# Dense steps up to sixty slots ahead of their target, in place of sixteen, in a hand-planned FFN-attention-FFN kernel

## What is computed

```python
x = x + 0.5 * ffn(layernorm(x))      # r * (relu(k)^2 W_v), r = sigmoid(xr W_r), k = xk W_k
x = x + attention(layernorm(x))      # 16 heads of 16, rotary q and k, causal softmax
x = x + 0.5 * ffn(layernorm(x))
```

## Time and profile before

| | us |
|---|---|
| median of 3 runs | 3071.79 (3069.86 to 3072.07) |
| the profiled execution | 3073.15 |
| its span, first to last instruction | 3071.4 |
| TensorE products busy in it | 2945.7 |
| VectorE busy | 2531.8 |
| ScalarE busy | 2216.2 |
| POOL busy | 1573.0 |
| mean granted TensorE clock | 0.989 of full |

### The profile page before, as it was taken

One profiled execution on the slowest core, in us unless ns is written; L12 is line 12 of the kernel. 1 busy time (PEld: TensorE's weight loads), 2 busy tenths in 40 slices (PEclk: granted clock), 3 DMA queues, 4 the chain that ended last, 5 costly groups with the idle time before them and its releaser, 6 DMA issues.

```text
span 3071.4 us, 56193 instructions
## 1 busy us (share of the span) xinstructions
PE 2945.7 (96%) x18245; PEld 1670.0 (54%) x18245; DVE 2531.8 (82%) x7302; ACT 2216.2 (72%) x4802; POOL 1573.0 (51%) x2190
## 2 busy tenths in 40 slices
PE   6899999999999999999999999999999999999997
PEld 4454555555555555555555555555555555555444
DVE  3788887888888888888888888888888898888872
ACT  4477776777777777777777777777777777777764
POOL 5455454555555554465555555455454554555323
PEclk9899999999999999999999999999999999999998
DMA  3433443443444343453443443434453543443421
GB/s 100 81 67 73 76 101 64 88 83 76 91 72 91 76 85 74 80 99 65 88 79 71 102 77 81 84 73 85 78 98 61 101 81 66 96 76 76 84 58 39
DMA packets 202584, 245.48 MB, mean 80 GB/s; under 512 B 68405, under 2 KB 104245, under 8 KB 202293
## 3 DMA queue, kind: packets, MB, share of 16 engines
q1 hardware_dynamic: 202293, 241.90, 40.3%
HBM read 53.48 MB, written 51.38 MB: 34 GB/s over the span
## 4 chain that ended last, share of the span: by engine, by line
PE 70%; DVE 21%; issue 3%; ACT 3%; POOL 1%; SPq 1%; DMA 1%; POOLq 0%; DVEq 0%; ACTq 0%
PE ps_y L954 14%; PE ps_s L923 13%; PE ps_m L933 12%; PE ps_d L1010 6%; PE ps_d L1013 6%; PE ps_d L1007 6%; DVE ps_m L1162 5%; PE ps_d L1019 4%; PE ps_d L1000 3%; DVE mx_sb L1165 3%; PE ps_d L1023 2%; PE ps_d L961 2%; DVE ka_sb L1187 2%; DVE qb_sb L1220 2%; ACT pt_sb L1049 1%
## 5 line engine op out<-in xcount | busy, mean ns | idle before, releaser
L1049 ACT ACTIVATE pt_sb<-ps_s 128x512 f32<-128x512 f32 (+1 forms) x3039 | 1460.3, 491 | 676.1 <-PE ps_s L923 645.7
L1162 DVE CUSTOM_DVE_ANT_0 ps_m<-ps_m,mask_sb 128x128 f32<-128x128 f32 (+3 forms) x2048 | 995.5, 497 | 275.7 <-PE ps_m L933 252.9
L933 PE MATMUL ps_m<-kr_sb,qr_sb 96*128 96x512 bf16 (+3 forms) x3072 | 1003.4, 330 | 55.5 <-DVE mx_sb L1162 44.8
L923 PE MATMUL ps_s<-qr_sb,kr_sb 99*128 99x512 bf16 (+1 forms) x3039 | 994.5, 330 | 23.1 <-ACT pt_sb L1049 14.3
L1165 DVE TENSOR_REDUCE mx_sb<-ps_m 128x1 f32<-128x512 f32 x1024 | 700.9, 684 | 130.6 <-PE ps_m L933 124.7
L1294 POOL TENSOR_SCALAR_AFFINE_SELECT pt_sb<-pt_sb 128x512 f32<-128x512 f32 x512 | 339.8, 664 | 820.3 <-ACT pt_sb L1049 819.6
L954 PE MATMUL ps_y<-pt_sb,v_sb 128*32 128x512 f32 (+3 forms) x6144 | 591.5, 495 | 4.5 <-POOL pt_sb L1294 3.3
L923 PEld LDWEIGHTS ps_s<-qr_sb,kr_sb 99*128 99x128 bf16 x3039 | 292.6, 96 | 440.9 <-issue 238.0
L933 PEld LDWEIGHTS ps_m<-kr_sb,qr_sb 96*128 96x128 bf16 x3072 | 302.2, 98 | 381.4 <-DVE mx_sb L1162 114.5
L1007 PE MATMUL ps_d<-ka_sb,wk_sb 128*128 128x256 f32 x1024 | 314.5, 394 | 2.4 <-DVE dif_sb L1199 2.0
L1019 PE MATMUL ps_d<-axn_sb,wqk_sb 128*128 128x256 f32 x1024 | 310.5, 389 | 3.8 <-ACT axn_sb L1091 3.8
(11 more groups left out here) (96 smaller groups left out, 3537.2 us busy)
## 6 DMA issues: line engine op xcount, KB each, us to landing
kr_sb<-part_sb SPq DMA_DIRECT2D x378, 128.0 KB, 4.5
qr_sb<-part_sb SPq DMA_DIRECT2D x378, 128.0 KB, 5.0
y_way<-yt_sb SPq DMA_DIRECT2D x128, 256.0 KB, 2.7
sw_sb<-qb_sb SPq DMA_DIRECT2D x496, 64.0 KB, 2.0
x_sb<-x SPq DMA_DIRECT2D x64, 256.0 KB, 4.1
yn_sb<-y_way SPq DMA_DIRECT2D x64, 256.0 KB
den_sb<-r_way SPq DMA_DIRECT2D x64, 256.0 KB
out<-x_sb SPq DMA_DIRECT2D x64, 256.0 KB, 2.2
```

The costliest lines, as they stand in the source:

```text
L923: eng.matmul(score_bank(slot)[:, 0:width], kr_sb[0:KR + NP, n % RS, j, kb * P:(kb + 1) * P], qr_sb[0:KR + NP, n % RS, j, q0:q0 + width], s ...
L933: eng.matmul(ps_m[:, u % NM, 0:width], qr_sb[0:KR, n % RS, j, i * P:(i + 1) * P], kr_sb[0:KR, n % RS, j, piece * QC:piece * QC + width], s ...
L1049: eng.activation(pt_sb[:, buffer, j, column:column + width], score_bank(slot)[:, 0:width], ACT.Exp, scale=SCALE).then_inc(exped, 1)
L1162: eng.tensor_tensor_reduce(ps_m[:, u % NM, 0:width], ps_m[:, u % NM, 0:width], mask_sb[:, m0:m0 + width], 1.0, -3e38, ALU.add, ALU.max, be ...
```

## The change

`EARLY`, the number of slots by which a dense step of rank group 2 may stand ahead of its target, goes from 16 to 60. It is used in one place, `step()`, and holds for both planners. Nothing else is changed.

```diff
     UNIT = 4 * CH / GHZ
     TICK = 900
-    EARLY = 16
+    EARLY = 60
```

## The result

| | before | after |
|---|---|---|
| median, same chip, 4 runs each, us | 3071.93 (3069.86 to 3074.42) | 3130.95 (3129.51 to 3132.89) |
| span of the profiled execution | 3071.4 | 3131.2 |
| mean granted TensorE clock | 0.989 | 0.983 |

The change makes the kernel slower by 59.0 us: ratio 1.0195, interval [1.0182, 1.0207].

A forecast was written before the change was run, and what follows sets the result against it. The prediction took the slot-by-slot interlock of TensorE's and VectorE's lists as the bound. Its terms, 0 - 10.8 + 3.8 - 4.2 + 2.9 = -8.3 us, gave a forecast of 3064 us, range 3036 to 3096.

The forecast's parts named there:

- Step 1: Steady batches: holes filled before the second FFN reopen later at about the same unit price; change 0.
- Rival A: Dense steps: POOL and VectorE collide more, +22 us, 3087 us; L1187 mean over 0.70 us for, under 0.68 against; chance 0.24.
- Step 2: Dense work moves up to 44 slots ahead, 36 units from the last batches into the start, 0.30 us each: -10.8 us.
- Steps 3 and 4: Start: moved FFN units partly uncovered on VectorE, +3.8 us; second pair's rope steps, -4.2 and +2.9 us.
- Step 4 (b): Start: second pair's rope swap, cosine, sine and addition may delay VectorE's first maximum: 0 to +5.8, taken as +2.9 us.
- 4 (a): Start: earlier rope product 4 lets the L862 DMAs releasing the first score begin sooner, before 82 us: -4.2 us.
- Rival B: Whole kernel: dependences hold steps in place, or costs in the start eat the shift; +2.1 us, 3074 us; chance 0.22.
- Rival C: Steady batches: runs of slots without a unit come apart, letting VectorE catch up; 33 us faster, 3032 us; chance 0.12.

The follow-up runs named there:

- the two holds: POOL's dense steps wait, from one slot before VectorE's five short maxima steps, until these end: before 3043.97 us; sixty from slot 48 only 3044.34 us.
- at 32: Bound of 32 from slot 48 on, sixteen in the start, with POOL's wait one slot before the five maxima steps: 3056.05 us against 3069.86 before.
- the bound by clocks: Kernel before with sixty slots only in the planner by clocks (slot 48 on), sixteen kept in the start: 3121.93 us against 3071.23.
- the hold in after: Changed kernel with POOL's dense steps waiting, from one slot before the five short maxima steps, until these end: 3059.23 us against 3069.76 before.
- the hold and sixteen in the start: Sixty from slot 48 on only, with POOL's wait one slot before the five maxima steps: 3044.34 us against 3069.76 before.
- the rope steps alone: Kernel before with sixty slots in the start for the rope steps only, sixteen for everything else: 3088.25 us against 3069.86.
- the FFN steps alone: Kernel before with sixty slots in the start for FFN and attention norm steps only: 3078.18 us against 3069.86.
- the fills: Kernel before with twelve write-only POOL fills of a spare tile per head group, beside the five maxima steps: 3137.44 us against 3069.86.
- the reading steps: Kernel before with six short POOL products per head group that read SBUF, beside the five maxima steps: 3173.46 us against 3069.76.

## Why the prediction was wrong

**Step 1 ("steady batches: 0") is the step that failed.** It argued by units: as many holes open as are filled, at one price. That part held between sixteen and sixty, as the two holds show (365.5 against 365.8 us for two batches), though not at 32, 12 us worse. What it left out is that the list also fixes what POOL does while VectorE runs its rows of short steps. The ten batches 4 to 13, which it put at 0, grew by 42.7 us; the bound by clocks cost 50.7 us in all, and with the hold in both kernels 0.4 us of it is left.

**Rival A had the mechanism and the sign, and the wrong place.** It priced collisions where they were easy to see, in L1187 and L1193, and set the mean of L1187 as its sign. That mean is 0.648 us, under the 0.68 that spoke against A, while A was happening in five lines that it left out, as small steps of 128x32 or less. What the change does to such a step reaches TensorE: VectorE's next maximum stands behind the last of the five in its queue, and TensorE's next product waits for it. (That a dense mix has slack in front of its user was not measured.) At +45 us of VectorE the price was also twice the +22 given. The Trainium skill's page "SBUF — State Buffer", section "SBUF: two separate sides", says that the shared port goes to whoever starts first, for its whole instruction, where VectorE's has two SBUF inputs and POOL's reads SBUF. By that rule a step of 0.18 us costs as much as the POOL step ahead of it; the traces agree, with 1.25 us beside a POOL step of 1.28.

**Step 2 (shift, -10.8)** had the count and about the right size per unit. The lists have 35 more units ahead of slot 0, and 28 fewer in batch 14, at 0.30 us each with the hold in after (0.35 with the hold and sixteen in the start). There -8.5 us would have come, but only -2.0 showed in after, which the hold turned into -8.5. The end of the kernel gained almost nothing more (-1.0 us).

**Steps 3 and 4 (+3.8, -4.2, +2.9: +2.5 in all)** were mis-sized. Step 4 (b) looked at one chain, POOL's cosine for rope product 4, and put the worst at 5.8 us for the first maximum. It came 19.4 us later, as rope steps 4 and 5 and a whole FFN chunk got ahead of it. The gain of 4 (a) did not come: the L862 DMAs began at 104.17 us, not before 82, since the maxima that they need were late. Slot 0 came 26.3 us later. With sixty in the start alone the units already done returned 16.3 us of it in batch 0, which step 2 counted only at the end, and the net was +10.4 us. No run parts steps 3 and 4 cleanly: the rope steps alone cost 18.4 us, the FFN steps alone 8.3.

Rival B (no change) fell with the 59 us, though its thought that the start eats the shift was near. Rival C's holes came apart only in part (by the lists a steady batch has 8 slots in runs of five or more, where before had 25 in two batches), and its 33 us are not there even with the blocking gone: the bound alone is worth 0.4 us then.

## What to carry to other kernels

A reordering is also a change of what runs side by side. Before you price one at nothing, list the shortest dependent steps on the path and compare the mean of each with its minimum: one row of five tiny steps, at 2.27 us where about 1.0 would do, was worth 26 us before anything was changed. Hold the other engine's long steps back *before* the row begins; a wait in the same slot was too late and gave 7.3 of 25.8 us and 12.8 of 69.5. When a queue is in order, more freedom in the start lets work with a later deadline in front of the first instruction of the critical path.

## What the hardware showed that I had not expected

- VectorE steps of 0.17 to 0.19 us took up to 1.25 us beside POOL's 128x512 float32 steps, five in a row 4.8 us. This held not only for those with two SBUF inputs but for the TENSOR_SCALAR of L1252 with one (751 ns on average after, 727 before, 248 in after with the hold) and, less often, the CAST of L1257 (333 ns before, 222 after, 182 in after with the hold). The Trainium skill's page "SBUF — State Buffer", in the same section "SBUF: two separate sides", counts VectorE's faster two-port modes among what is shut out; that these two steps run in one, no run here shows.
- Fills on POOL, which only write, left the later two steps with two inputs short (L1254 and L1259 of before; the first, L1248, kept 573 ns, 590 in before). In the kernel with the fills:

```profile
L1257 DVE SCALAR_TENSOR_TENSOR mres_sb<-mx_sb,mp_sb 128x32 f32<-128x32 f32 x64 | 13.1, 205 | 2.2
```

  beside 368 ns with the reading steps and 274 in before (line L1254 there). Part of the drop from 274 may come from POOL's own reading steps having moved away. The one-input TENSOR_SCALAR was not short with the fills: 817 ns, 727 in before.
- POOL, busy for 51% of the span, was not free to be late. Extra work of 3.75 us a group cost 68 us, while a hold of about 1 us a group, which shortened the row, gained 26. Why its lateness costs so much was not followed to the end.
- After 3.15 us without products the granted clock read 0.62 for the next 4.5 us, a mix of the levels of 1.2 and 2.4 GHz.
